# Attention with exact maxima: value products of two key tiles together, three score and three maximum banks, keys and values fetched in paced pieces

## The chip, the cores and the metric

One core of one Trainium2 chip runs the kernel. The metric is the time of one execution in microseconds (us). The kernel is the whole of a conditioned transformer block; the change is inside its attention stage.

## What is computed

Two sequences of 2048 rows of 512 channels pass through RMS norm with a conditioned shift and scale, 16-head attention (32 channels a head, rotary positions, no mask), and a gated feed-forward part, all float32:

```
qkv = h @ w_qkv + b_qkv
q, k = _rope(q), _rope(k)                  # heads of 32
attn = softmax(q k^T / sqrt(32)); out = attn @ v
x = x + out @ w_ao + b_ao
```

## The kernel before

Stage A writes rotated queries and keys (as a high and a low part that add up) and values to DRAM. Stage B, `stage_b` (line 472), is the attention; C and D are the output projection and the feed-forward part. B works in 32 **units** (`UNITS`): a unit is one group of four heads (`GH`, eight groups) and one block of 512 queries, four units to a group. A unit has 16 key tiles (`kt`) of 128 keys, and a loop of four rounds holds eight units written out (`run`, line 535).

For each tile and head PE makes a **score** matmul (`scores`, line 792: 128 keys by 512 queries into a bank of `ps_s`), ScalarE takes its exponential into the ring `pt` (line 656, eight tiles, `RING`), and four matmuls of 32 columns side by side, one per head, make the **value products** (PV, line 844) into `ps_o`. Softmax's maxima are made one unit ahead: a **maximum** matmul (line 767) gives 128 queries by 512 keys into a bank of `ps_m`, and VectorE reduces it (line 717). So a unit has 64 scores and 64 maxima, in the order `ORDER` = "smsmmsms" per key tile (s a score, m a maximum), and PV behind each such eight. There are `LEAD` = 2 score banks and `EARLY` = 4 maximum banks, one bank for `ps_o` and one for `ps_d`. A score waits until the exponential two before it is done (`p_ready`), a maximum until the reduction four before it is done (`max_done`).

The denominators are sums over all keys. POOL adds the ring's tiles into `acc` in pairs: `first_pair` (line 681) adds tiles 0 and 1; for the other seven pairs (`PAIRS`) `fold_pair` issues a DMA that adds the even tile onto the odd one inside the ring (line 688, 1 MB), when PV of the odd tile is done, and `add_pair` adds that into `acc` when the DMA has landed (line 695). POOL's order in a unit is: first pair, last add of the unit before, fold 0, fold 1, add 0, fold 2, add 1, and so on to fold 6, add 5. ScalarE may write tile kt into the ring only when `slot_free` says so: the add of the pair that lay there is done (`pool_added`). PE turns `acc` into denominators behind PV of tile 7 of the next unit (line 776, `D_AT`); at tile 10 (`TURN`) it transposes the finished maxima (line 786), which go through DRAM into the queries' last rows for the next unit.

SP's queue issues in each unit (`body`): queries of the unit after next (three transfers, 0.75 MB), then in the first unit of a group two of the next group's three key transfers (1 MB each), in the second the third, in the third the values (1 MB); then the output, the denominators, the maxima and the reciprocals.

## Time and profile before

| | us |
|---|---|
| median of three runs | 3688.61 (3687.13 to 3688.67) |
| the profiled execution | 3684.44 |
| its span, first to last instruction | 3682.6 |
| PE busy | 3247.0 (88%) |
| VectorE, POOL, ScalarE busy | 2028.4, 1660.1, 1573.8 |
| mean granted TensorE clock | 0.933 |

PE is TensorE's matmuls, PEld its weight loads, DVE VectorE, ACT ScalarE. b_ names are stage B's: b_s and b_m are the score and maximum banks, b_o the value products, b_d the denominators, b_pt the ring, b_acc the sums. A bracket behind an instruction is the idle time of its engine before it and what ended it. A value product of one key tile is eight instructions, which the timeline shows as one row.

### The profile page before, as it was taken

What the parts mean: (1) busy time and instruction counts of PE and PEld (TensorE: products, weight loads), DVE (VectorE), ACT (ScalarE), POOL (GpSimd) and SP (SyncE); (2) the same over time, 40 slices, a digit from 0 to 9 for tenths busy, and PEclk for the clock granted to TensorE, in tenths of its full rate; (3) what the DMA queues carried; (4) which work ended last, traced back from release to release, by engine and by line L of the source; (5) the groups of instructions that cost most, each with busy time, mean ns of one, the idle gap of its engine ahead of it and who ended that gap; (6) DMA issues with size and microseconds to landing.
All of it is one profiled execution on the core that took longest, in us unless ns stands there. A gap on an engine that the chain in (4) does not pass through costs nothing. (4 is left out here: it accounts for less than half of the span.)

```text
span 3682.6 us, 53143 instructions
## 1 busy us (share of the span) xinstructions
PE 3247.0 (88%) x15180; PEld 2087.6 (57%) x15180; DVE 2028.4 (55%) x3254; ACT 1573.8 (43%) x2848; POOL 1660.1 (45%) x732
## 2 busy tenths in 40 slices
PE   5888699999998998989999997444799999799999
PEld 5666544444444444444444443333588888688887
DVE  2878587777777776768777765434321222321222
ACT  1343226666666666657666664233211111211111
POOL 0222228877777777778877777655100000100000
PEclk9999869999999999999999998767899999899999
DMA  4444548887887878878887876654421120421210
GB/s 163 143 142 143 141 102 180 168 177 164 182 178 163 178 167 174 178 168 183 170 169 170 183 169 138 187 183 160 160 92 46 55 81 12 149 92 46 84 53 23
DMA packets 177578, 507.93 MB, mean 138 GB/s; under 512 B 25338, under 2 KB 42858, under 8 KB 143086
## 3 DMA queue, kind: packets, MB, share of 16 engines
q0 software_dynamic: 36240, 248.53, 33.1%
q1 hardware_dynamic: 130580, 233.58, 21.6%
q10 hardware_dynamic: 10512, 22.81, 1.9%
q8 instruction: 121, 1.98, 0.2%
q14 instruction: 125, 1.02, 0.1%
HBM read 175.18 MB, written 93.62 MB: 73 GB/s over the span
## 5 line engine op out<-in xcount | busy, mean ns | idle before, releaser
L717 DVE TENSOR_REDUCE b_mpart<-b_m 128x1 f32<-128x512 f32 x2136 | 1328.5, 684 | 480.3 <-PE b_m L767 476.0
L656 ACT ACTIVATE b_pt<-b_s 128x512 f32<-128x512 f32 x2048 | 1116.5, 596 | 625.4 <-PE b_s L792 492.7
L695 POOL TENSOR_TENSOR b_acc<-b_acc,b_pt 128x2048 f32<-128x2048 f32 x225 | 1040.4, 4624 | 352.2 <-DMA b_pt<-b_pt 350.8
L792 PE MATMUL b_s<-b_qs,b_ks 98*128 98x512 f32 x2050 | 904.2, 441 | 91.5 <-ACT b_pt L656 80.4
L792 PEld LDWEIGHTS b_s<-b_qs,b_ks 98*128 98x128 f32 x2050 | 393.7, 192 | 752.1 <-ACT b_pt L656 669.5
L767 PE MATMUL b_m<-b_ks,b_qs 96*128 96x512 f32 x2136 | 794.9, 419 | 20.9 <-issue 20.6
L844 PE MATMUL b_o<-b_pt,b_vg 128*32 128x512 f32 x4096 | 557.5, 617 | 0.0
L767 PEld LDWEIGHTS b_m<-b_ks,b_qs 96*128 96x128 f32 x2136 | 424.2, 199 | 96.4 <-DVE b_mpart L717 26.3
L1229 DVE SCALAR_TENSOR_TENSOR d_uf<-d_a,keep_chan,d_sg 128x512 f32<-128x512 f32 x128 | 96.1, 751 | 578.2 <-PE d_a L1257 578.2
L1181 POOL DMA_DIRECT2D d_raw<-in_w_fc x32 | 24.0, 755 | 592.1 <-POOLq L1106 495.7
L1200 ACT ACTIVATE d_sg<-d_g,keep_chan 128x512 f32<-128x512 f32 x128 | 88.0, 688 | 420.0 <-PE d_g L1257 420.0
L1203 ACT ACTIVATE d_u_hi<-d_uf 128x512 fp32r<-128x512 f32 x128 | 80.9, 632 | 433.8 <-DVE d_uf L1229 433.8
L1257 PE MATMUL d_g<-d_h_hi,d_w_hi 128*128 128x512 f32 x512 | 201.1, 393 | 45.8 <-DVE d_w_lo L1218 45.8
L341 POOL TENSOR_TENSOR a_qc<-a_q,early_cos 128x512 f32<-128x512 f32 x64 | 92.4, 1444 | 328.2 <-ACT a_q L307 297.3
L688 POOL DMA_DIRECT2D b_pt<-b_pt x224 | 201.5, 919 | 44.0 <-PE b_o L844 40.4
L1257 PE MATMUL d_g<-d_h_lo,d_w_hi 128*128 128x512 f32 x512 | 200.8, 392 | 0.0
L1257 PE MATMUL d_g<-d_h_hi,d_w_lo 128*128 128x512 f32 x512 | 200.8, 392 | 0.0
L1257 PE MATMUL d_a<-d_h_hi,d_w_hi 128*128 128x512 f32 x512 | 199.2, 389 | 0.0
L1257 PE MATMUL d_a<-d_h_hi,d_w_lo 128*128 128x512 f32 x512 | 199.2, 389 | 0.0
L1270 PE MATMUL d_y<-d_w_hi,d_u_hi 128*128 128x512 f32 x512 | 199.2, 389 | 0.0
L1270 PE MATMUL d_y<-d_w_hi,d_u_lo 128*128 128x512 f32 x512 | 199.2, 389 | 0.0
L1270 PE MATMUL d_y<-d_w_lo,d_u_hi 128*128 128x512 f32 x512 | 199.2, 389 | 0.0
(130 smaller groups left out, 3606.3 us busy)
## 6 DMA issues: line engine op xcount, KB each, us to landing
b_pt<-b_pt POOLq DMA_DIRECT2D x225, 1024.0 KB, 8.0
b_ks<-scratch_qk_hi SPq DMA_DIRECT2D x18, 1024.0 KB, 13.8
b_qs<-scratch_qk_hi SPq DMA_DIRECT2D x68, 256.0 KB, 6.0
scratch_qk_hi<-a_q_hi SPq DMA_DIRECT2D x64, 256.0 KB, 2.4
scratch_qk_lo<-a_q_lo SPq DMA_DIRECT2D x64, 256.0 KB, 2.8
d_h_hi<-scratch_h_hi SPq DMA_DIRECT2D x16, 1024.0 KB, 7.4
d_h_lo<-scratch_h_lo SPq DMA_DIRECT2D x16, 1024.0 KB, 9.6
d_y<-scratch_y SPq DMA_DIRECT2D x16, 1024.0 KB, 7.9
```

Of the source, the lines that this page charges most:

```text
L341: pool.tensor_tensor(qc[:, t % 2, :], q[:, t % 2, :], cos[:, bass.ds(it * TB, TB)], ALU.mult).then_inc(qc_ready, 1)
L656: act.activation(pt[:, kt % RING, h, :], ps_s[:, i % LEAD, :], ACT.Exp, scale=SCALE).then_inc(p_ready, 1)
L688: pool.dma_start(pt[:, kt % RING, :, :], pt[:, (kt - 1) % RING, :, :], accum_op=ALU.add).then_inc(pair_in[(PAIRS * j + n) % 2], 16)
L695: pool.tensor_tensor(acc[slot][:], acc[slot][:], pt[:, (2 * n + 3) % RING, :, :], ALU.add).then_inc(pool_added, 1)
L717: dve.tensor_reduce(mpart[slot][:, i // 4, i % 4:i % 4 + 1], ps_m[:, i % EARLY, :], AX.X, ALU.max).then_inc(max_done, 1)
L767: pe.matmul(ps_m[:, i % EARLY, :], qs[qslot][0:KR, h, s * P:(s + 1) * P], ks[kslot][0:KR, h, k * TB:(k + 1) * TB], start=True, stop=True). ...
L792: pe.matmul(ps_s[:, i % LEAD, :], ks[kslot][0:QR, h, kt * P:(kt + 1) * P], qs[qslot][0:QR, h, :], start=True, stop=True).then_inc(st_done, 1)
L844: last = pe.matmul(ps_o[h * HD:(h + 1) * HD, 0, :], vg[kslot][:, kt, h * HD:(h + 1) * HD], pt[:, kt % RING, h, :], start=kt == 0, stop=kt ...
L1200: act.activation(sg[:, f % 2, :], ps_g[:, f % 2, :], ACT.Silu, bias=chan[:, t:t + 1]).then_inc(sg_ready, 1)
L1229: dve.scalar_tensor_tensor(uf[:, f % 2, :], ps_a[:, f % 2, :], chan[:, t:t + 1], sg[:, f % 2, :], ALU.add, ALU.mult).then_inc(uf_ready, 1)
L1257: last = pe.matmul(ps[:, f % 2, :], w[:, f, t, k, :], h[s][:, k, :], start=i == 0, stop=i == 3 * KT - 1)
L1270: last = pe.matmul(ps_y[:, i, :], u[:, f % 2, i * P:(i + 1) * P], w[:, f, :], start=f == 0 and n == 0, stop=f == NF - 1 and n == 2)
```

## The change

1. PV of an even tile is left for the odd one: PE runs through sixteen scores and maxima, then makes both tiles' value products.
2. `LEAD` 2 to 3, `EARLY` 4 to 3. `bank(i)` gives item i of a unit its bank (i mod 3, and bank 1 for item 63), `before(i)` the item that had the bank last.
3. POOL issues fold 0 of a unit ahead of the last add of the unit before.
4. `slot_free`: an even tile's slot is free when the fold that read it has landed (`pair_in`), without waiting for the add; in the first unit of eight, where the pair belongs to the unit before, it still waits for the add.
5. Keys and values come in pieces of half a megabyte (two heads' keys, or eight tiles' values): `load_piece` gives unit j pieces 3(j mod 4) to 3(j mod 4) + 2 of eight; the first goes out when PV of three tiles of the unit is done, the second at six, the third behind the maxima. The output's store moves ahead of them.

```diff
@@ -465,8 +465,18 @@
 PAIRS = NK // 2 - 1
 ADDS = PAIRS + 1
 RING = 8
-LEAD = 2
-EARLY = 4
+LEAD = 3
+EARLY = 3
+def bank(i):
+    return i if i < 0 else 1 if i % 64 == 63 else i % 64 % 3
+def before(i):
+    return {0: -4, 1: -1, 2: -2, 63: 61}.get(i, i - 3)
 def stage_b(nc, io, keep, scratch):
@@ -543,12 +553,22 @@
             sp.sem_inc(d_out, 16)
             sp.sem_inc(r_out, 16 * GH)
-            def load_keys(G, i, r):
+            def load_keys(G, i, r, half):
                 src = qk_hi if r != 1 else qk_lo
-                sp.dma_start(f32(ks[i][r * HD:(r + 1) * HD, :, :]), src[1, G]).then_inc(k_in[i], 16)
-
-            def load_values(G, i):
-                sp.dma_start(vg[i][:], scratch["v"][G]).then_inc(v_in[i], 16)
+                heads = slice(GH // 2 * half, GH // 2 * (half + 1))
+                sp.dma_start(f32(ks[i][r * HD:(r + 1) * HD, heads, :]), src[1, G][:, heads, :]).then_inc(k_in[i], 16)
+            def load_values(G, i, half):
+                part = slice(NK // 2 * half, NK // 2 * (half + 1))
+                sp.dma_start(vg[i][:, part, :], scratch["v"][G][:, part, :]).then_inc(v_in[i], 16)
+            def load_piece(j, G, i, step):
+                piece = 3 * (j % 4) + step
+                if piece < 6:
+                    load_keys(G, i, piece // 2, piece % 2)
+                elif piece < 8:
+                    load_values(G, i, piece % 2)
             def load_queries(G, c, i):
                 for r, src in enumerate((qk_hi, qk_hi, qk_lo)):
...
@@ -594,17 +616,15 @@
                 sp.wait_ge(st_done, STEPS * (u + 1))
                 load_queries((2 * pair + (j + 2) // 4) % NG, (j + 2) % 4, (j + 2) % 4)
                 nG, ni = (2 * pair + j // 4 + 1) % NG, (j // 4 + 1) % 2
-                if j % 4 == 0:
-                    load_keys(nG, ni, 0)
-                    load_keys(nG, ni, 1)
-                if j % 4 == 1:
-                    load_keys(nG, ni, 2)
-                if j % 4 == 2:
-                    load_values(nG, ni)
                 G, c = (2 * pair + (j + 7) // 4 + NG - 2) % NG, (j + 3) % 4
                 store_output(u, G, c)
+                sp.wait_ge(pv_done, NK * u + RING - 1 + 3)
+                load_piece(j, nG, ni, 0)
+                sp.wait_ge(pv_done, NK * u + RING - 1 + 6)
+                load_piece(j, nG, ni, 1)
                 spread_denominators(u)
                 load_maxima(u + 1, (j + 1) % 2, (j + 1) % 4)
+                load_piece(j, nG, ni, 2)
                 store_reciprocals(u, G, c)
             run(sp, body)
...
@@ -635,11 +655,17 @@
                 act.wait_ge(d_out, 16 * (u + 1))
                 act.activation(d_sb[:], ps_d[:, 0, :], ACT.Copy).then_inc(d_read, 1)
-            def slot_free(u, kt):
+            def slot_free(u, kt, pair, j):
                 act.wait_ge(pv_done, NK * u + kt + 1)
                 old = (kt - RING) % NK
-                if old >= 2:
+                if old >= 2 and old % 2 == 0:
+                    g = PAIRS * (j if kt >= RING else j - 1) + old // 2 - 1
+                    if g >= 0:
+                        act.wait_ge(pair_in[g % 2], 16 * (PAIRS * 4 * pair + g // 2 + 1 + g % 2))
+                    else:
+                        act.wait_ge(pool_added, added(u - 1, old // 2 - 1))
+                elif old >= 2:
                     act.wait_ge(pool_added, added(u if kt >= RING else u - 1, old // 2 - 1))
                 else:
                     act.wait_ge(pool_added, ADDS * u + ADDS + 1)
@@ -649,11 +675,11 @@
             def body(u, pair, j):
                 for kt in range(NK):
-                    slot_free(u, kt)
+                    slot_free(u, kt, pair, j)
                     for h in range(GH):
                         i = GH * kt + h
                         act.wait_ge(st_done, STEPS * (u + 1) + i + 1)
-                        act.activation(pt[:, kt % RING, h, :], ps_s[:, i % LEAD, :], ACT.Exp,
+                        act.activation(pt[:, kt % RING, h, :], ps_s[:, bank(i), :], ACT.Exp,
                                        scale=SCALE).then_inc(p_ready, 1)
                         if kt == 0 and h == LEAD - 1:
                             read_products(u)
@@ -696,8 +722,8 @@
             def body(u, pair, j):
                 first_pair(u, j % 2)
+                fold_pair(u, j, pair, 0)
                 add_pair(u - 1, j - 1, pair, PAIRS - 1, (j + 1) % 2)
-                fold_pair(u, j, pair, 0)
                 for n in range(1, PAIRS):
                     fold_pair(u, j, pair, n)
                     add_pair(u, j, pair, n - 1, j % 2)
@@ -714,7 +740,7 @@
             def maxima(n, slot, lo, hi):
                 for i in range(lo, hi):
                     dve.wait_ge(max_ps, ITEMS * n + i + 1)
-                    dve.tensor_reduce(mpart[slot][:, i // 4, i % 4:i % 4 + 1], ps_m[:, i % EARLY, :], AX.X, ALU.max).then_inc(max_done, 1)
+                    dve.tensor_reduce(mpart[slot][:, i // 4, i % 4:i % 4 + 1], ps_m[:, bank(i), :], AX.X, ALU.max).then_inc(max_done, 1)
             def finish_max(n, slot):
                 dve.wait_ge(max_done, ITEMS * (n + 2))
@@ -763,8 +789,8 @@
                 for i in range(lo, hi):
                     h, s, k = i // 16, i // 4 % 4, i % 4
-                    pe.wait_ge(max_done, ITEMS * (n + 1) + i + 1 - EARLY)
-                    pe.matmul(ps_m[:, i % EARLY, :], qs[qslot][0:KR, h, s * P:(s + 1) * P],
+                    pe.wait_ge(max_done, ITEMS * (n + 1) + before(i) + 1)
+                    pe.matmul(ps_m[:, bank(i), :], qs[qslot][0:KR, h, s * P:(s + 1) * P],
                               ks[kslot][0:KR, h, k * TB:(k + 1) * TB], start=True, stop=True).then_inc(max_ps, 1)
             def denominators(u, slot):
@@ -779,7 +805,7 @@
             def operands(j, pair):
                 pe.wait_ge(q_in[j % 4], 48 * (2 * pair + j // 4 + 1))
-                pe.wait_ge(k_in[j // 4 % 2], 48 * (pair + j // 8 + 1))
+                pe.wait_ge(k_in[j // 4 % 2], 96 * (pair + j // 8 + 1))
             def turn_max(n):
                 pe.wait_ge(mneg_ready, n + 1)
@@ -788,8 +814,8 @@
             def scores(n, kslot, qslot, i):
                 kt, h = i // GH, i % GH
-                pe.wait_ge(p_ready, STEPS * (n + 1) + i + 1 - LEAD)
-                pe.matmul(ps_s[:, i % LEAD, :], ks[kslot][0:QR, h, kt * P:(kt + 1) * P], qs[qslot][0:QR, h, :],
+                pe.wait_ge(p_ready, STEPS * (n + 1) + before(i) + 1)
+                pe.matmul(ps_s[:, bank(i), :], ks[kslot][0:QR, h, kt * P:(kt + 1) * P], qs[qslot][0:QR, h, :],
                           start=True, stop=True).then_inc(st_done, 1)
             for i in range(SUB):
@@ -835,15 +861,18 @@
                     if kt == TURN:
                         pe.wait_ge(d_read, u + 2)
                         turn_max(u + 1)
-                    if kt == 0:
+                    if kt % 2 == 0:
+                        continue
+                    if kt == 1:
                         pe.wait_ge(o_read, u + 1)
                         if j % 4 == 0:
-                            pe.wait_ge(v_in[kslot], 16 * (pair + 1))
-                    pe.wait_ge(p_ready, STEPS * (u + 1) + GH * (kt + 1))
-                    for h in range(GH):
-                        last = pe.matmul(ps_o[h * HD:(h + 1) * HD, 0, :], vg[kslot][:, kt, h * HD:(h + 1) * HD],
-                                         pt[:, kt % RING, h, :], start=kt == 0, stop=kt == NK - 1)
-                    last.then_inc(pv_done, 1)
+                            pe.wait_ge(v_in[kslot], 32 * (pair + 1))
+                    for n in (kt - 1, kt):
+                        pe.wait_ge(p_ready, STEPS * (u + 1) + GH * (n + 1))
+                        for h in range(GH):
+                            last = pe.matmul(ps_o[h * HD:(h + 1) * HD, 0, :], vg[kslot][:, n, h * HD:(h + 1) * HD],
+                                             pt[:, n % RING, h, :], start=n == 0, stop=n == NK - 1)
+                        last.then_inc(pv_done, 1)
                     if kt == D_AT:
                         denominators(u, (j + 1) % 2)
```

**Order of the instructions, PE, at an even tile's end** (L791/L792 and in the change L817/L818 are scores, L766/L767 and L792/L793 maxima, L844 and L873 value products; ISA rows set up a wait). Before:

```order
L767 MATMUL b_m<-b_ks,b_qs 128x512
L791 ISA
L792 MATMUL b_s<-b_qs,b_ks 128x512
L842 ISA
L844 MATMUL b_o<-b_pt,b_vg 32x512 x4
L791 ISA
L792 MATMUL b_s<-b_qs,b_ks 128x512
L766 ISA
L767 MATMUL b_m<-b_ks,b_qs 128x512
```

Of the change, from an even tile's last score to the next tile's first maximum:

```order
L793 MATMUL b_m<-b_ks,b_qs 128x512
L817 ISA
L818 MATMUL b_s<-b_qs,b_ks 128x512
L817 ISA
L818 MATMUL b_s<-b_qs,b_ks 128x512
L792 ISA
L793 MATMUL b_m<-b_ks,b_qs 128x512
```

and at the odd tile's end:

```order
L818 MATMUL b_s<-b_qs,b_ks 128x512
L871 ISA
L873 MATMUL b_o<-b_pt,b_vg 32x512 x4
L871 ISA
L873 MATMUL b_o<-b_pt,b_vg 32x512 x4
L817 ISA
L818 MATMUL b_s<-b_qs,b_ks 128x512
```

The value products between the two tiles have gone behind those of the odd tile; scores and maxima keep their order.

**POOL, at a unit's start** (L681/L707 the first pair, L688/L714 a fold, L695/L721 an add). Before:

```order
L681 TENSOR_TENSOR b_acc<-b_pt 128x2048
L693 ISA
L694 ISA
L695 TENSOR_TENSOR b_acc<-b_acc,b_pt 128x2048
L686 ISA
L688 DMA b_pt<-b_pt 128x2048
L686 ISA
L688 DMA b_pt<-b_pt 128x2048
```

Of the change:

```order
L707 TENSOR_TENSOR b_acc<-b_pt 128x2048
L712 ISA
L714 DMA b_pt<-b_pt 128x2048
L719 ISA
L720 ISA
L721 TENSOR_TENSOR b_acc<-b_acc,b_pt 128x2048
L712 ISA
L714 DMA b_pt<-b_pt 128x2048
```

The first fold now stands ahead of the add, the second behind it.

## Rows read from the trace of the kernel before

**Rows 1.** The page: busy time by engine (section 1).
```profile
PE 3247.0 (88%) x15180; PEld 2087.6 (57%) x15180; DVE 2028.4 (55%) x3254; ACT 1573.8 (43%) x2848; POOL 1660.1 (45%) x732
```

**Rows 2.** Stretches: length, busy PE, PEld, DVE, ACT, POOL, clock, DMA share, GB/s.
```profile
887.80:938.60 50.80, 50.80 (x268) 24.52 (x267) 40.63 (x69) 35.66 (x67) 40.85 (x15) 1.00 0.80 167
1150.20:1211.30 61.10, 51.04 (x249) 24.79 (x248) 38.12 (x64) 33.65 (x63) 43.39 (x16) 0.89 0.84 173
...
519.00:2274.00 1755.00, 1663.78 (x8475) 802.37 (x8473) 1300.54 (x2174) 1145.03 (x2110) 1347.95 (x478) 0.97 0.83 172
```

**Rows 3.** Timeline of PE: start, us, instruction; one key tile, then the denominators.
```profile
1002.02 0.50 PE L792 MATMUL b_s<-b_qs,b_ks 98*128 98x512 f32 x1
1002.36 0.39 PE L767 MATMUL b_m<-b_ks,b_qs 96*128 96x512 f32 x1
1002.60 0.39 PE L792 MATMUL b_s<-b_qs,b_ks 98*128 98x512 f32 x1
...
1003.78 0.42 PE L792 MATMUL b_s<-b_qs,b_ks 98*128 98x512 f32 x1
1004.13 1.06 PE L844 MATMUL b_o<-b_pt,b_vg 128*32 128x512 f32 x8
1005.13 0.50 PE L792 MATMUL b_s<-b_qs,b_ks 98*128 98x512 f32 x1
...
1032.23 1.06 PE L844 MATMUL b_o<-b_pt,b_vg 128*32 128x512 f32 x8
1033.11 1.04 PE L776 MATMUL b_d<-b_acc,keep_ones 128*32 128x512 f32 x8
```

**Rows 4.** Waits of the stage, 520 to 2274 us: total, times, longest.
```profile
POOL b_acc L695 <- DMA b_pt<-b_pt: 348.5, 159, 9.1
...
ACT b_pt L656 <- POOL b_acc L695: 85.0, 22, 10.4
```

**Rows 5.** Timeline of POOL: an undisturbed unit's seam, then a stall.
```profile
899.60 0.87 POOL L688 DMA_DIRECT2D b_pt<-b_pt  x1
...
910.31 4.59 POOL L695 TENSOR_TENSOR b_acc<-b_acc,b_pt 128x2048 f32<-128x2048 f32 x1 [0.18 <-DMA b_pt<-b_pt]
...
1171.45 0.86 POOL L688 DMA_DIRECT2D b_pt<-b_pt  x1
...
1190.60 4.49 POOL L695 TENSOR_TENSOR b_acc<-b_acc,b_pt 128x2048 f32<-128x2048 f32 x1 [9.14 <-DMA b_pt<-b_pt]
1195.04 1.75 POOL L688 DMA_DIRECT2D b_pt<-b_pt  x2
```

**Rows 6.** DMA of the stage: queue, packets, MB, share; issues, us to landing.
```profile
q0 software_dynamic: 32000, 233.06, 66.3%
q1 hardware_dynamic: 35430, 66.52, 15.7%
...
b_pt<-b_pt POOLq DMA_DIRECT2D x223, 1024.0 KB, 8.0
```

**Rows 7.** Timelines of DVE, ACT and PEld over the tile of rows 3.
```profile
1002.79 2.49 DVE L717 TENSOR_REDUCE b_mpart<-b_m 128x1 f32<-128x512 f32 x4 [0.62 <-PE b_m L767]
...
1002.56 2.27 ACT L656 ACTIVATE b_pt<-b_s 128x512 f32<-128x512 f32 x4 [0.83 <-PE b_s L792]
...
1003.21 0.19 PEld L792 LDWEIGHTS b_s<-b_qs,b_ks 98*128 98x128 f32 x1 [0.19 <-ACT b_pt L656]
```

**Rows 8.** Timelines of DVE and PEld in the first maxima.
```profile
501.61 2.47 DVE L717 TENSOR_REDUCE b_mpart<-b_m 128x1 f32<-128x512 f32 x4
...
502.94 0.28 PEld L767 LDWEIGHTS b_m<-b_ks,b_qs 96*128 96x128 f32 x1 [0.31 <-DVE b_mpart L717]
```

**Rows 9.** Stretch at a low clock, and PE's timeline there.
```profile
480.00:520.00 40.00, 39.44 (x73) 19.59 (x76) 38.94 (x67) 3.35 (x7) 0.00 (x0) 0.50 0.29 62
...
518.83 0.63 PE L767 MATMUL b_m<-b_ks,b_qs 96*128 96x512 f32 x1
519.26 0.63 PE L792 MATMUL b_s<-b_qs,b_ks 98*128 98x512 f32 x1
```

More of the change, by code:

```diff
@@ L583, in _ @@
             load_queries(0, 0, 0)
-            for r in range(3):
-                load_keys(0, 0, r)
-            load_values(0, 0)
+            for half in range(2):
+                for r in range(3):
+                    load_keys(0, 0, r, half)
+            for half in range(2):
+                load_values(0, 0, half)
             sp.wait_ge(ones_ready, 1)
@@ L618, in _ @@
                 sp.wait_ge(q_in[i], 48 * (UNITS // 4 + 1))
-            sp.wait_ge(k_in[0], 48 * (NG // 2 + 1))
-            sp.wait_ge(v_in[0], 16 * (NG // 2 + 1))
+            sp.wait_ge(k_in[0], 96 * (NG // 2 + 1))
+            sp.wait_ge(v_in[0], 32 * (NG // 2 + 1))
         @block.scalar
```

## The prediction

> **What bounds the kernel now.** I read the page first: TensorE is busy in 88% of the span, no other engine in over 55% [rows 1]. The change touches only the attention stage, so I then asked for that stage: from 519 to 2274 us it is 1755 us for 32 units, **54.8 us each**, with PE at 95% of it, VectorE 74%, ScalarE 65%, POOL 77%, the DMA engines at 83% [rows 2]. Two units side by side tell what the 54.8 is made of [rows 2]: from 887.8 to 938.6 there is one unit in 50.8 us and PE never stops; from 1150.2 to 1211.3 the same unit takes 61.1 us, with the granted clock at 0.89. So 32 x (54.8 - 50.8) = 128 us are stalls, the rest is PE's own beat.
>
> The beat, in order of time [rows 3]: a score or maximum matmul every 0.23 us, 0.35 from the last score to the value products (PV), 1.00 from PV to the next score, and 0.34 instead of 0.23 to the matmul behind that. One key tile takes 1005.13 - 1002.02 = 3.11 us. Sixteen of them are 49.8; the denominators add 0.88 (1033.11 - 1032.23 [rows 3]) and the maximum's transpose 0.2: 50.8, as the undisturbed unit shows.
>
> The stalls: the waits of the stage put 85.0 us on ScalarE waiting for POOL's adds, 22 times, up to 10.4 us, and 348.5 us on POOL waiting for the folding DMA [rows 4]. The timeline of one shows why [rows 5]. The last fold of a unit is issued at 1171.45, its add starts at 1190.60: 19.2 us to land, where the median is 8.0 [rows 6]. In that stretch the SP queue has put out 0.75 MB of queries and 2 MB of keys. In the undisturbed unit of rows 2, which begins with queries alone, it is 899.60 to 910.31, 10.7 us. POOL stands idle for 9.14 us with the next unit's fold 0, long ready, queued behind that add; then it issues two folds at once (1195.04) and waits again. ScalarE's slot for key tile 6 is freed by that add alone, which ends at 1190.60 + 4.49 = 1195.09; this is the wait of 10.4 us [rows 4]. PE follows.
>
> **The change, part by part.** (1) PV of two key tiles together. Per two key tiles one passage in and out of PV falls away. One PV with its passage is 0.35 + 1.00 + 0.34 = 1.69 us. In the place of the first of two, scores and maxima now run on (two steps of 0.23), and its product costs, behind or ahead of the other, what the denominators cost behind a PV, 0.88 to 0.91 (I take 0.91): 1.69 - 0.46 - 0.91 = 0.3 saved. Two tiles by PE alone: 6.22 - 0.3 = **5.9 us**. That is the gain if nobody makes PE wait, 8 x 0.3 = 2.5 us a unit.
>
> (2) The maximum banks go from four to three, while eight maxima now come in one burst without the rest that PV gave. This is what I think decides the time, and it follows from four distances: VectorE starts a reduction 0.43 us after its matmul (1002.36 to 1002.79), reductions follow at (2.48 - 0.68) / 3 = 0.60 us [rows 7], and a matmul that waits for a bank starts 0.74 us after the reduction that frees it started (in the first maxima, where PE runs behind VectorE: reductions start at 501.61 and 502.21, and the weights of a waiting maximum at 502.94, 0.73 to 0.74 behind the second [rows 8]). ScalarE's are 0.45, 0.50 and 0.65 (1002.56 to 1003.21) [rows 7]. Put down from the first score at 0, matmuls at the beat of rows 3: m0 0.34, m1 0.80, m2 1.04, m3 1.51, m4 2.21, m5 2.67, m6 2.91, m7 3.37, the next score at 5.9; scores at 0, 0.57, 1.27, 1.74, 1.97, 2.44, 3.14, 3.61. Reductions d0 to d7: 0.77, 1.37, 1.97, 2.57, 3.17, 3.77 and on. m5 needs d2 + 0.74 = 2.71 (hardly late), m6 needs d3 + 0.74 = 3.31 instead of 2.91, m7 needs d4 + 0.74 = 3.91 instead of 3.77. So the last score stands at 4.14, PV at 4.49, 4.49 + 0.91 + 1.00 = 6.40; each late maximum also loads its weights uncovered, as the matmul behind PV does, 0.1 more (0.34 against 0.23). Between **6.38 and 6.50 I take 6.45 us** for two tiles: slower than 6.22. During the double PV VectorE has finished d7 by about 5.0 and idles, so nothing is made up. With four banks all these waits would vanish (m6 would need d2 + 0.74 = 2.71).
>
> The same walk for the three score banks: exps at 0.54, 1.04, 1.73, 2.22, 2.72; the latest demand is score 7, at 2.72 + 0.65 = 3.37, before its place at 4.14. So the third score bank costs nothing and covers PV (three exps are 1.8 us against 1.9 of PV). Banks are numbered so that items 63 and 1 have two banks instead of three: for the maxima m7 of tiles 8 and 9 then needs d5, 0.6 us later, once a unit. The transpose in the middle of a pair is hidden by the wait of m6.
>
> Unit without stalls: 8 x 6.45 + 0.9 + 0.6 = **53.1 us against 50.8: +2.3**.
>
> (3) Fold 0 goes ahead of the last add of the unit before, and even slots are freed when the fold that read them has landed rather than after the add. Fold 0 can be issued when PV of tile 3 is done, 2 x 6.45 = 12.9 us into the unit, and takes 0.9; the last fold goes out when PV of tile 15 is done, at about the unit's start, and beside queries alone lands 10.7 us later, so it is no longer the last to be waited for. The add ends at 12.9 + 0.9 + 4.6 = 18.4 us (4.6: rows 5). ScalarE needs it for tile 7, whose first score (28) is the second one behind three double tiles: 3 x 6.45 + 0.57 + 0.45 = 20.4 us, 2.0 us to spare. Tile 6 (score 24, at 12.9 + 2.44 + 0.45 = 15.8 us) now needs only the landing. Each us of landing past about 15.8 shows on PE.
>
> (4) Keys and values in eight half-megabyte pieces a group instead of four transfers, the first two of a unit behind PV of tiles 3 and 6, the third behind the maxima. The bytes stay. Nothing on SP is waited for before tile 10: its denominators come at tile 8, its maxima at 11, so the two new waits (tiles 3 and 6) hold up nothing behind them. Half pieces could cost more engine time: the SP queue takes 15.7% of 1755 us for 66.5 MB, 4.1 us per MB [rows 6]. The 1 MB of a unit could cost between nothing more and the same 4.1 us again (a half as dear as a whole), nearer to nothing, since half of that queue's bytes come in 256 KB transfers already (1 of 2 MB a unit). Two queues' 45 us plus 4.1 are 92% of a unit, so either is hidden. The Trainium skill (DMA: Bandwidth & Descriptors, Rules for kernel authors) wants at least 1 MiB in a DMA for full rate and so speaks against the halves; by it the pieces would load the queue more, and in the sum nothing would change unless the folds land later.
>
> Stalls that stay: in the first of eight units the even slots still wait for the add (tile 6 at 15.8 us, add done at 18.4: 2.6 / 8 = 0.3 us a unit). Between 0 and the 4.0 of now I take this 0.3, since the three causes seen in [rows 5] (a 2 MB burst, fold 0 queued behind, the add as the release) are each taken away.
>
> **Sum.** 32 x (53.1 + 0.3 - 54.8) = -45 us. The profiled execution took 3684.4; the median of the runs is 3688.6, 4.2 more. 3688.6 - 45 = **3644 us**. The first maxima run on VectorE's 0.60 with three banks as with four ((0.74 + 0.43) / 3 = 0.39 us, and 0.53 with the 0.43 doubled for a halved clock, both under 0.60), and all other stages are as before.
>
> **Rivals.**
> - *Reductions keep up* and the pair takes 5.9: 8 x 5.9 + 0.9 + 0.2 = 48.3. The two DMA queues take (66.3 + 15.7)% of 54.8 = 45.0 us a unit [rows 6], 93% of that, so folds land later and some waits stay: 49.5, 32 x 5.3 = 170, 3519 us. Against it: it needs reductions at under 0.47 us, they come at 0.60. Chance 0.08.
> - *The stalls stay* (slower). If the last fold, now in the queue with fold 0, lands as late as before, ScalarE waits at tile 7 instead of 6. Then the longer beat is all there is: 32 x 2.3 = +74, 3762 us. It decides from 2.3 - 4.0, i.e. once more than 1.7 us of stalls a unit are left. For it: beside queries alone the last fold already takes 10.7 us, 2.7 above the median, and now a half megabyte of the unit before may still be in front of them. Against: the undisturbed unit of rows 2 began with queries too. Chance 0.11.
> - *The clock falls* (slower). From 480 to 520 us the weight loads of the maxima stood idle 0.31 of each 0.60 us for a reduction, and the granted clock was 0.50, the 1.2 GHz level [rows 8, 9]; a score then took its place every 0.43 us instead of 0.23 [rows 9]. A pair at that level costs 16 x 0.2 + 2 x 0.9 less the waits that it covers, about 4.4 us more. One pair in eight: 32 x 4.4 = 141 more, 3785 us; one in 25 eats the gain. Against: PE still works 5.9 of 6.45 us. The Trainium skill (TensorE: Matmul & The Clock Gate, A second HAM failure mode) tells of a kernel whose short waits on PSUM banks made the clock swing between its levels, which is this case's shape; here it is at 0.50 in the first maxima and part of the time in the stalled unit (0.89), while the undisturbed unit keeps 1.00 [rows 2]. Chance 0.04.
> - *It doesn't do what it says*, e.g. the pacing waits are already met (the count starts at 7): the wait asks 7 + 3, so they hold. Even then the keys only come as now. No chance of its own.
>
> **How the numbers follow.** The forecast has 0.77. Its own range: 6.38 to 6.50 a pair is -18 to +13 us, stalls of 0 to 1 us a unit -10 to +22: 3616 to 3679. For 8 in 10 I reach some way to both sides: **3590 to 3695**, which leaves out most of the two slow rivals and the fast one. Under 0.2%, 7 us, a change can't be told from none here. Faster: 0.77 + 0.08 less a tail of 0.04, **0.81**; same **0.04**; slower **0.15**.
>
> **What would show it.** Right: maxima's weight loads idle before two or three matmuls of eight, put down to VectorE; two tiles in 6.4 to 6.5 us; gaps of 5 to 10 us on PE behind ScalarE gone; fold landings under 14 us; DMA share about 85%. Wrong: pairs of 5.9 (my bank walk fails), ScalarE still waiting for POOL for 50 us or more (the reordering fails), or a granted clock under 0.95 in the stage.

## The result, and the profile after

| | before | changed |
|---|---|---|
| median of four runs, us | 3688.6 (3687.1 to 3689.7) | 3644.4 (3642.6 to 3647.2) |
| the profiled execution | 3684.4 | 3647.2 |
| its span | 3682.6 | 3645.4 |
| mean granted TensorE clock | 0.933 | 0.946 |

The ratio is 0.9901, with a 95% interval of 0.9878 to 0.9924: 44 us faster, against a forecast of 45.

The page of the changed kernel, busy time by engine, beside [rows 1]:

```profile
PE 3249.6 (89%) x15181; PEld 2092.3 (57%) x15181; DVE 2003.0 (55%) x3254; ACT 1590.4 (44%) x2848; POOL 1670.0 (46%) x732
```

There is nothing to see there: every engine does what it did. Stretches of the stage, with the columns of [rows 2], tell more; the first is the stage, the second one unit:

```profile
540.00:2240.00 1700.00, 1646.60 (x8378) 796.90 (x8376) 1261.19 (x2151) 1147.53 (x2086) 1350.68 (x474) 0.99 0.84 178
1000.00:1053.00 53.00, 51.91 (x267) 25.25 (x267) 39.86 (x69) 36.33 (x67) 42.71 (x15) 1.00 0.90 192
```

PE is busy in 97% of the stage, but an undisturbed unit now has PE idle for 1.1 of its 53.0 us, where before it had none in 50.8 [rows 2]. The timeline of PE, one pair of key tiles, against [rows 3] (start, us, instruction; L818 scores, L793 maxima, L873 value products, L802 denominators):

```profile
1001.70 1.92 PE L873 MATMUL b_o<-b_pt,b_vg 128*32 128x512 f32 x16
1003.55 0.50 PE L818 MATMUL b_s<-b_qs,b_ks 98*128 98x512 f32 x1
...
1006.34 1.01 PE L793 MATMUL b_m<-b_ks,b_qs 96*128 96x512 f32 x2
...
1007.45 0.50 PE L793 MATMUL b_m<-b_ks,b_qs 96*128 96x512 f32 x1
...
1008.12 1.92 PE L873 MATMUL b_o<-b_pt,b_vg 128*32 128x512 f32 x16
...
756.39 1.04 PE L802 MATMUL b_d<-b_acc,keep_ones 128*32 128x512 f32 x8
809.40 1.04 PE L802 MATMUL b_d<-b_acc,keep_ones 128*32 128x512 f32 x8
```

Two tiles take 1008.12 - 1001.70 = 6.42 us. The last two rows are one unit apart, 53.0 us, and the units between the loop's ends are all 53.0. Weight loads in the same pair:

```profile
1005.06 0.19 PEld L793 LDWEIGHTS b_m<-b_ks,b_qs 96*128 96x128 f32 x1 [0.29 <-DVE b_mpart L743]
...
1006.25 0.19 PEld L793 LDWEIGHTS b_m<-b_ks,b_qs 96*128 96x128 f32 x1 [0.17 <-DVE b_mpart L743]
1006.85 0.19 PEld L793 LDWEIGHTS b_m<-b_ks,b_qs 96*128 96x128 f32 x1 [0.41 <-DVE b_mpart L743]
...
1007.45 0.19 PEld L793 LDWEIGHTS b_m<-b_ks,b_qs 96*128 96x128 f32 x1 [0.30 <-DVE b_mpart L743]
```

These are maxima m3, m5, m6 and m7 of the eight; each waits for VectorE. m7 starts 1007.45 - 1003.55 = 3.90 us behind the first score. The waits of the stage (total, times, longest), beside [rows 4]:

```profile
PEld b_m L793 <- DVE b_mpart L743: 282.9, 903, 0.9
...
POOL b_acc L721 <- DMA b_pt<-b_pt: 140.9, 122, 3.3
...
ACT L682 <- issue: 20.0, 3, 7.2
...
ACT b_pt L682 <- POOL b_acc L721: 13.0, 4, 4.2
```

ScalarE's waits for POOL have gone from 85.0 us to 13.0, POOL's for its folds from 348.5 to 140.9, and waits of PE's weight loads for VectorE have come in. The seam between two units on POOL, against [rows 5]:

```profile
1059.30 0.86 POOL L714 DMA_DIRECT2D b_pt<-b_pt  x1
...
1064.44 4.86 POOL L707 TENSOR_TENSOR b_acc<-b_pt 128x2048 f32<-128x2048 f32 x1
1070.09 0.87 POOL L714 DMA_DIRECT2D b_pt<-b_pt  x1 [0.78 <-PE b_o L873]
1070.70 4.87 POOL L721 TENSOR_TENSOR b_acc<-b_acc,b_pt 128x2048 f32<-128x2048 f32 x1
```

The last fold goes out at 1059.30, fold 0 at 1070.09 with only PE's value products to wait for, and the last add follows without a wait. The queues' shares, against [rows 6]:

```profile
q0 software_dynamic: 32096, 233.85, 67.8%
q1 hardware_dynamic: 37046, 67.99, 15.4%
...
b_pt<-b_pt POOLq DMA_DIRECT2D x223, 1024.0 KB, 8.0
b_ks<-scratch_qk_hi SPq DMA_DIRECT2D x32, 512.0 KB, 5.1
```

A fold's median stays at 8.0 us. The SP queue took 15.4% of 1720 us for 68.0 MB, 3.9 us per MB where it was 4.1, so no cost of the halves is to be seen. The Trainium skill (DMA: Bandwidth & Descriptors, Rules for kernel authors) wants 1 MiB and more in a DMA for the most bandwidth. No run here measures a DMA's rate by itself, but the queue's engine time per MB did not rise.

### The profile page after: what moved, and what is told of

Its sections match the earlier page's. It is cut to its first block and busy times, and to the rows that moved or that the text cites. A ratio compares the mean times of both kernels' runs of the same rounds, so it can differ in the third digit from the quotient of the medians.

```text
span 3645.4 us, 53309 instructions
## 1 busy us (share of the span) xinstructions
PE 3249.6 (89%) x15181; PEld 2092.3 (57%) x15181; DVE 2003.0 (55%) x3254; ACT 1590.4 (44%) x2848; POOL 1670.0 (46%) x732
## 5 line engine op out<-in xcount | busy, mean ns | idle before, releaser
L743 DVE TENSOR_REDUCE b_mpart<-b_m 128x1 f32<-128x512 f32 x2136 | 1306.2, 683 | 469.7 <-PE b_m L793 469.6
L682 ACT ACTIVATE b_pt<-b_s 128x512 f32<-128x512 f32 x2048 | 1132.5, 601 | 540.2 <-PE b_s L818 504.0
L721 POOL TENSOR_TENSOR b_acc<-b_acc,b_pt 128x2048 f32<-128x2048 f32 x225 | 1054.7, 4687 | 143.5 <-DMA b_pt<-b_pt 143.3
L793 PE MATMUL b_m<-b_ks,b_qs 96*128 96x512 f32 x2136 | 899.5, 452 | 51.7 <-issue 20.1
L818 PE MATMUL b_s<-b_qs,b_ks 98*128 98x512 f32 x2051 | 821.9, 417 | 23.3 <-ACT b_pt L682 19.6
L793 PEld LDWEIGHTS b_m<-b_ks,b_qs 96*128 96x128 f32 x2136 | 413.4, 194 | 371.6 <-DVE b_mpart L743 312.4
L818 PEld LDWEIGHTS b_s<-b_qs,b_ks 98*128 98x128 f32 x2051 | 391.1, 191 | 322.4 <-issue 208.1
L873 PE MATMUL b_o<-b_pt,b_vg 128*32 128x512 f32 x4096 | 492.5, 598 | 0.0
L714 POOL DMA_DIRECT2D b_pt<-b_pt x224 | 195.3, 872 | 205.7 <-PE b_o L873 188.4
L873 PEld LDWEIGHTS b_o<-b_pt,b_vg 128*32 128x32 f32 x4096 | 106.8, 109 | 247.7 <-issue 184.2
L1286 PE MATMUL d_a<-d_h_lo,d_w_hi 128*128 128x512 f32 x512 | 199.2, 389 | 0.0
```

Source lines behind the costliest of these rows:

```text
L682: act.activation(pt[:, kt % RING, h, :], ps_s[:, bank(i), :], ACT.Exp, scale=SCALE).then_inc(p_ready, 1)
L714: pool.dma_start(pt[:, kt % RING, :, :], pt[:, (kt - 1) % RING, :, :], accum_op=ALU.add).then_inc(pair_in[(PAIRS * j + n) % 2], 16)
L721: pool.tensor_tensor(acc[slot][:], acc[slot][:], pt[:, (2 * n + 3) % RING, :, :], ALU.add).then_inc(pool_added, 1)
L743: dve.tensor_reduce(mpart[slot][:, i // 4, i % 4:i % 4 + 1], ps_m[:, bank(i), :], AX.X, ALU.max).then_inc(max_done, 1)
L793: pe.matmul(ps_m[:, bank(i), :], qs[qslot][0:KR, h, s * P:(s + 1) * P], ks[kslot][0:KR, h, k * TB:(k + 1) * TB], start=True, stop=True).th ...
L818: pe.matmul(ps_s[:, bank(i), :], ks[kslot][0:QR, h, kt * P:(kt + 1) * P], qs[qslot][0:QR, h, :], start=True, stop=True).then_inc(st_done, 1)
```

## The experiments

The changed kernel agrees with the forecast in its beat, but a sum can come out right by two errors. So the parts were run apart, and then what was left. Ratios are to the kernel before on the same chip, with 95% intervals; a unit's length is the time from one unit's denominators to the next one's. The kernel before took 3685.4 (beside e1 to e4), 3684.0 (e5 to e8) and 3688.7 us (e9 to e12 and the changed kernel's own runs 3688.6), so differences of medians across these are good to some 4 us. e1's maxima leave out half of the keys, so its output is another one; only its time is of use. All others compute the whole block.

| kernel | us | ratio |
|---|---|---|
| e5 pieces alone | 3691.2 | 1.0016 [1.0000, 1.0032] |
| e12 slots alone | 3728.1 | 1.0107 [1.0071, 1.0144] |
| e2 fold 0 first alone | 3649.9 | 0.9903 [0.9881, 0.9924] |
| e9 fold 0 first, slots | 3612.4 | 0.9796 [0.9762, 0.9830] |
| e6 fold 0 first, pieces | 3611.3 | 0.9795 [0.9756, 0.9833] |
| e3 fold 0 first, slots, pieces | 3579.9 | 0.9716 [0.9700, 0.9732] |
| e4 merging and banks alone | 3693.6 | 1.0019 [1.0002, 1.0036] |
| the whole change | 3644.4 | 0.9901 [0.9878, 0.9924] |
| e10 whole change, banks 2 and 4 | 3622.2 | 0.9827 [0.9793, 0.9861] |
| e7 whole change, other order | 3579.9 | 0.9721 [0.9686, 0.9756] |
| e1 whole change, half reductions | 3582.7 | 0.9720 [0.9701, 0.9740] |
| e8 as e3, no loop | 3550.5 | 0.9636 [0.9602, 0.9670] |
| e11 as e7, no loop | 3548.8 | 0.9625 [0.9592, 0.9659] |

### Which resource sets the pair of tiles: e1, e10, e7

e1 shortens the reductions:

```diff
-                                       scale=SCALE).then_inc(p_ready, 1)
+                                       scale=SCALE / 64).then_inc(p_ready, 1)
...
-                    dve.tensor_reduce(mpart[slot][:, i // 4, i % 4:i % 4 + 1], ps_m[:, bank(i), :], AX.X, ALU.max).then_inc(max_done, 1)
+                    dve.tensor_reduce(mpart[slot][:, i // 4, i % 4:i % 4 + 1], ps_m[:, bank(i), 0:TB // 2], AX.X, ALU.max).then_inc(max_done, 1)
```

> The changed kernel, but VectorE reduces only 256 of the 512 columns of each maximum matmul (so the maxima are those of half the keys, and the exponent is scaled by 1/64 to stay finite): the same instructions, shorter reductions. Theory (three banks and a reduction every 0.60 us hold PE up at the sixth to eighth maximum of a pair): the reductions then follow at about 0.34 us, no maximum waits, two key tiles fall from the 6.42 us measured after the change to 5.9, and a unit from 53.0 to 48.5 to 50.6, where folds start to hold it: 3500 to 3575 us. Rival (the second pair of value products or the three score banks set the 6.42): two tiles stay at 6.3 to 6.4 us, 3630 to 3645 us.

Measured: 3582.7 us, 8 above the theory's range. PE's timeline, three value products behind one another:

```profile
1005.25 1.92 PE L873 MATMUL b_o<-b_pt,b_vg 128*32 128x512 f32 x16
...
1011.17 1.93 PE L873 MATMUL b_o<-b_pt,b_vg 128*32 128x512 f32 x16
...
1017.00 1.92 PE L873 MATMUL b_o<-b_pt,b_vg 128*32 128x512 f32 x16
```

and from the waits of its stage:

```profile
PE b_s L818 <- DMA b_qs<-scratch_m: 30.0, 19, 2.3
...
PEld b_m L793 <- DVE b_mpart L743: 15.1, 31, 0.5
```

The first pair, 5.92 us, has the maxima's transpose in it; the second, without it, takes 5.83. In the changed kernel both kinds take 6.42. Nothing is altered in time but the reductions' length, and the weight loads' waits for VectorE fell from 282.9 to 15.1 us. So VectorE behind three banks sets the 6.42. The fastest units are 48.6 us, but most are 50 to 54: with the shorter beat the maxima's way through DRAM and the folds come late.

e10 puts two score and four maximum banks back, in a kernel that still merges:

```diff
-LEAD = 3
-EARLY = 3
...
+LEAD = 2
+EARLY = 4
...
-                    pe.wait_ge(max_done, ITEMS * (n + 1) + before(i) + 1)
...
+                    pe.wait_ge(max_done, ITEMS * (n + 1) + i + 1 - EARLY)
...
-                pe.wait_ge(p_ready, STEPS * (n + 1) + before(i) + 1)
...
+                pe.wait_ge(p_ready, STEPS * (n + 1) + i + 1 - LEAD)
```

> The changed kernel with the banks put back: two for scores, four for maxima, value products still two tiles together. Theory by the same walk: no maximum waits any more, but a score now waits for the exponential two before it; score 4 starts at 1.73 + 0.65 = 2.37 instead of 1.97 and everything behind it moves, 6.3 to 6.4 us for two tiles instead of 6.42; the extra 0.6 us of the bank numbering goes: 52.0 to 52.5 a unit, 3610 to 3635 us. Weight loads of scores wait for ScalarE, those of maxima for nobody. Rival (the four maximum banks are all that counts): 5.9 for two tiles, 3590 us or less.

Measured: 3622.2 us, units of 52.0. Its PE timeline:

```profile
999.68 1.92 PE L863 MATMUL b_o<-b_pt,b_vg 128*32 128x512 f32 x16
...
1003.29 0.42 PE L808 MATMUL b_s<-b_qs,b_ks 98*128 98x512 f32 x1
1003.91 0.50 PE L808 MATMUL b_s<-b_qs,b_ks 98*128 98x512 f32 x1 [0.20 <-ACT b_pt L672]
...
1006.02 1.92 PE L863 MATMUL b_o<-b_pt,b_vg 128*32 128x512 f32 x16
```

The pair is 6.34 us, and score 4 starts 0.62 us after score 3 instead of 0.23, released by ScalarE: the other side binds, where the walk put it. Two tiles with separate value products take 2 x 3.11 = 6.22 us [rows 3], and merged ones 5.83 when nobody waits (e1). So either split of six banks costs more than merging brings; 3 and 3 takes 22 us more than 2 and 4.

e7 keeps 3 and 3 and changes one string:

```diff
-        ORDER, TURN = "smsmmsms", 10
+        ORDER, TURN = "msmssmsm", 10
```

> The changed kernel with one string altered: the order of scores and maxima in a tile is msmssmsm instead of smsmmsms. The first maximum then starts at 0 behind the value products instead of 0.34, two maxima never stand side by side within a tile, and the last one of a pair is the last matmul before the value products, so that it may start at 0.54 + 4 x 0.60 + 0.74 = 3.68 us, its natural place. Theory: two tiles 5.9 to 6.1 us instead of 6.42, units of 49 to 50.5 with some waits for folds, 3560 to 3595 us. Rival (the three banks bind whatever the order): 6.3 or more for two tiles, 3625 us or above.

Measured: 3579.9 us, 64.5 less than the changed kernel. Its PE timeline:

```profile
1003.47 1.92 PE L873 MATMUL b_o<-b_pt,b_vg 128*32 128x512 f32 x16
1005.33 0.50 PE L793 MATMUL b_m<-b_ks,b_qs 96*128 96x512 f32 x1
...
1009.43 1.92 PE L873 MATMUL b_o<-b_pt,b_vg 128*32 128x512 f32 x16
```

The pair is 5.96 us. Three banks nearly suffice if the maxima are spread over the pair and VectorE is started at once behind the value products. The maxima's weight loads still wait 217.9 us in the stage for VectorE, against 282.9, but the pair is only 0.13 us longer than e1's.

### What took the stalls: e2, e5, e12, e6, e9, e3

e2 is one swap in POOL's order:

```diff
-                add_pair(u - 1, j - 1, pair, PAIRS - 1, (j + 1) % 2)
                 fold_pair(u, j, pair, 0)
+                add_pair(u - 1, j - 1, pair, PAIRS - 1, (j + 1) % 2)
```

> The kernel before with one part of the change alone: fold 0 issued ahead of the last add of the unit before. Theory (the stalls came from fold 0 being queued behind an add that waits for the landing of the last fold): most of the 4.0 us of stalls a unit go, PE keeps its own beat of 50.8: 50.8 to 51.5 a unit, 3565 to 3590 us, faster than the whole change. Rival (the 2 MB burst of keys delays the landings, and the order only moves the wait): units that begin with keys still stall by 8 us or more, 3650 us or above.

Measured: 3649.9 us, 60 above the theory's range and at the rival's bound: the swap alone is a third of what it brings with its two companions (e3 below). ScalarE's timeline tells the two reasons:

```profile
589.29 3.47 ACT L656 ACTIVATE b_pt<-b_s 128x512 f32<-128x512 f32 x6 [1.54 <-POOL b_acc L695]
...
803.19 1.09 ACT L656 ACTIVATE b_pt<-b_s 128x512 f32<-128x512 f32 x2 [7.86 <-POOL b_acc L695]
```

The first row comes back in nearly every unit, since the last add now stands behind fold 0 and ends just after ScalarE wants tile 6 (584.27 + 4.88 = 589.15); units are 51.5 us instead of 50.8. That is what freeing the slot at landing is good for. The second row is a fold that still lands late. It lies in unit 5 (counted from 0), which begins with 1 MB of keys, and not in unit 4, where the 2 MB go out; e9 shows why.

e5 is the pieces alone (`load_keys`, `load_values`, `load_piece`, the two waits on `pv_done` and the counts of the waits on keys and values, as in the change):

> The kernel before with the paced half-megabyte pieces alone. Theory (every unit that stalls has the last fold landing late and fold 0 queued behind it; the burst is only one of the causes): the long stalls of units that begin with 2 MB of keys shrink, those of the others stay or grow a little, as every unit but the fourth now has pieces: 53.5 to 55.5 us a unit, 3640 to 3700 us. Rival (the burst alone makes the stalls): 51.5 a unit or less, 3590 us or less.

Measured: 3691.2 us, within the theory's range, no gain. The waits of its stage, against [rows 4]:

```profile
POOL b_acc L705 <- DMA b_pt<-b_pt: 375.4, 167, 8.1
ACT b_pt L666 <- POOL b_acc L705: 87.7, 50, 4.6
```

As much waiting as before (87.7 against 85.0 us), in 50 waits instead of 22, none over 4.6. Pacing by itself spreads the stalls over the units.

e12 is `slot_free` alone:

```diff
...
-                if old >= 2:
+                if old >= 2 and old % 2 == 0:
+                    g = PAIRS * (j if kt >= RING else j - 1) + old // 2 - 1
+                    if g >= 0:
+                        act.wait_ge(pair_in[g % 2], 16 * (PAIRS * 4 * pair + g // 2 + 1 + g % 2))
+                    else:
+                        act.wait_ge(pool_added, added(u - 1, old // 2 - 1))
+                elif old >= 2:
...
```

> The kernel before with the slots freed at landing alone. Theory (the landing of the last fold and the fold 0 queued behind it are what is late; ScalarE's slots only tell when it shows): the stalls move by a tile, not away: 53.5 to 55.5 a unit, 3645 to 3700 us. Rival (the slots' rule is the main part of the gain): 3620 us or less.

Measured: 3728.1 us, slower than theory and rival had it. ScalarE's timeline at the start of unit 4, where 2 MB of keys go out:

```profile
752.18 1.08 ACT L662 ACTIVATE b_pt<-b_s 128x512 f32<-128x512 f32 x2 [7.74 <-DMA b_pt<-b_pt]
...
756.90 1.09 ACT L662 ACTIVATE b_pt<-b_s 128x512 f32<-128x512 f32 x2 [1.79 <-POOL b_acc L701]
```

Tile 6 starts at the landing, and one tile later ScalarE stops again for the add. Over the stage it waits 65.0 us for the folds' DMA and 61.5 for POOL, 126.5 together against 85.0. Before, a long unit is followed by an undisturbed one (62.5, 50.8, 58.9, 50.8 us for the fourth to seventh, counted between denominators); here the same four are all disturbed (60.5, 55.6, 57.3, 53.9). It looks as if the long stop used to let POOL catch up for the next unit; that is argued, no run isolates it.

e6 and e9 add one each of the two to the swap.

> Fold 0 first and paced pieces, without freeing the slots at landing; separate value products, two and four banks. It tells what the slots' rule adds to the version with all three (3580 us, 50.8 us a unit beside three back edges of 10 us). Theory (fold 0 alone left stalls of 8 to 10 us in the units with 2 MB or 1 MB of keys, which the pieces break up): 51.5 a unit as with fold 0 alone, no stall between the back edges, 3595 to 3615 us. Rival (the slots' rule does it, pieces nothing): units with stalls of 4 us and more, 3630 us or above.

> Fold 0 first and slots freed at landing, but keys and values in bursts of 2, 1 and 1 MB as before; separate value products, two and four banks. Against 3580 us with the pieces too. Theory (a landing later than about 15.8 us into the unit shows on PE, and beside 2 MB of keys the last fold takes up to 19): the units that begin with 2 MB of keys stall by 3 to 6 us, all others take 50.8: 3595 to 3625 us. Rival (with fold 0 first and free slots the burst is hidden): 3575 to 3585 us, the pieces buy nothing.

Measured: 3611.3 and 3612.4 us. e6 has units of 51.4 to 54.0 between the loop's ends, and no stop of PE there over 2 us. e9 has 50.7 to 51.6, and four of 56.0 to 59.5, each with one stop of PE of 3.6 to 5.5 us. The size is as expected (3 to 6), the place is not: the stops lie in units 5, 13, 21 and 29, which begin with 1 MB of keys, one unit behind those that begin with 2 MB. The one in unit 5:

```profile
797.02 1.08 ACT L662 ACTIVATE b_pt<-b_s 128x512 f32<-128x512 f32 x2 [6.39 <-DMA b_pt<-b_pt]
```

POOL in units 4 and 5:

```profile
751.12 4.57 POOL L701 TENSOR_TENSOR b_acc<-b_acc,b_pt 128x2048 f32<-128x2048 f32 x1 [8.26 <-DMA b_pt<-b_pt]
...
779.89 0.85 POOL L694 DMA_DIRECT2D b_pt<-b_pt  x1
...
797.09 4.55 POOL L701 TENSOR_TENSOR b_acc<-b_acc,b_pt 128x2048 f32<-128x2048 f32 x1 [4.85 <-DMA b_pt<-b_pt]
```

and SP's queue at the start of unit 5:

```profile
778.38 1.18 SPq L548 DMA_DIRECT2D b_ks<-scratch_qk_hi  x1
```

In unit 4 the last fold went out at 723.21, ahead of the queries and the 2 MB of keys (723.77 to 728.6), and nothing stopped. It was unit 4's own fold 0 (735.79) that took 15.3 us beside the burst, and POOL was late for the rest of the unit. So the last fold went out at 779.89, behind the queries and the 1 MB of keys of unit 5, and POOL took it up 17.2 us later. The times are the trace's; that the lateness is handed on in this way is our reading of them, and e6, where the pieces take the bursts away, agrees with it.

e3 has all three, and the value products, banks and beat of before:

> The kernel before with fold 0 first, the slots freed at landing and the paced pieces, but value products of each tile by themselves and two score and four maximum banks as before. Theory: only the loop's three back edges (6 to 7 us each) are left of the stalls: 50.8 to 51.2 a unit, 3560 to 3580 us, 65 to 85 us faster than the changed kernel, because merging with three banks costs 2.2 us a unit. Rival (merging pays, and the whole change needs its parts together): 3645 us or more.

Measured: 3579.9 us, as the theory has it. All units are 50.7 to 51.6 but those at the loop's ends. Its stage:

```profile
540.00:2180.00 1640.00, 1611.46 (x8378) 777.39 (x8377) 1283.77 (x2151) 1129.08 (x2087) 1349.26 (x476) 0.99 0.88 185
```

Against the kernel before on its own chip the swap takes 35 us off (e2), swap and pieces 73 (e6), swap and slots 76 (e9), all three 105 (e3). Without the swap the pieces add 7 us (e5) and the slots 39 (e12).

### Merging on its own: e4

This is the kernel before with the banks and the merged value products of the change, nothing else.

> The kernel before with the other half of the change: value products of two tiles together and three and three banks, nothing else. Theory: two tiles take 6.4 us, a unit without stalls 53.0; the slower PE gives POOL 2.2 us more a unit, so part of the old stalls vanish by themselves: 53.3 to 54.8 a unit, 3640 to 3690 us. Rival (stalls add to the longer beat as they stood): 57 us a unit, 3755 us.

Measured: 3693.6 us, 4 above the theory's range and far from the rival's. Its waits:

```profile
POOL b_acc L705 <- DMA b_pt<-b_pt: 257.4, 151, 8.9
...
ACT b_pt L666 <- POOL b_acc L705: 89.2, 27, 11.0
```

Undisturbed units are 53.0 here too, and more of them are undisturbed, as the slower beat gives POOL time; the long stalls stay, now mostly one unit behind the 2 MB of keys (9.9 us in units 5 and 21, 11.0 in unit 13). Added to e3 the same edit costs 3644.4 - 3579.9 = 64.5 us, 2.0 a unit.

### What was left: e8, e11

In the changed kernel the 32 units are 53.0 us but for three of 60.8 to 62.0, those over the loop's back edge, where every engine branches back to start the next round. ScalarE's timeline there:

```profile
945.65 1.28 ACT L682 ACT_TABLE_LOAD   x1 [5.89 <-issue]
```

It stands 5.89 us without a semaphore to wait for, and then loads its table again. The waits of the stage before [rows 4] had such a row too:

```profile
ACT L656 <- issue: 8.7, 2, 5.8
```

e8 is e3 with the loop of rounds written out, e11 is e7 with the same:

```diff
-            with eng.Fori(0, UNITS // 8) as pair:
+            for pair in range(UNITS // 8):
```

> The version without merging (3580 us) with the loop of four rounds written out, so that no engine branches back. Theory (ScalarE stands for 6 to 7 us at each back edge with no semaphore to wait for, and its table is loaded anew for 1.3 us, which with the low clock behind it costs 10 us a round): the three edges go, 3545 to 3560 us. Rival (fetching new instructions costs as much as branching back): 3575 to 3585 us, or slower if the straight code has to be fetched all the time.

> The changed kernel with the order msmssmsm and the loop written out. Theory: the 10 us a round that the back edges cost go, as in the version without merging (3580 to 3550 us): 3545 to 3555 us; the shorter beat of PE (49.7 us in its best units) is eaten by waits for the maxima's way through DRAM, which at 88% DMA share comes up to 2 us late. Rival (without the edges the merged version's shorter beat shows): 3535 us or less.

Measured: 3550.5 and 3548.8 us, 29.4 and 31.1 less than with the loop. e8's denominators at the place of the first edge, then e3's:

```profile
900.94 1.04 PE L792 MATMUL b_d<-b_acc,keep_ones 128*32 128x512 f32 x8
...
952.34 1.04 PE L792 MATMUL b_d<-b_acc,keep_ones 128*32 128x512 f32 x8
```

```profile
899.58 1.04 PE L792 MATMUL b_d<-b_acc,keep_ones 128*32 128x512 f32 x8
...
959.89 0.61 PE L792 MATMUL b_d<-b_acc,keep_ones 128*32 128x512 f32 x4
```

51.4 against 60.3 us. The branch and the reloading of the table go together in both, so how much of the cost is either's is not shown. These two are the fastest kernels of the study, 134 and 140 us below the kernel before on their own chips; they can't be told from each other. e11's best units are 49.8 us, but others take up to 53.1, with PE waiting up to 1.8 us for the maxima from DRAM, as the theory had it; e8's are 50.7 nearly throughout.

## Why the prediction was right

- **PE's beat and the stalls.** 54.8 us a unit were read as 50.8 of beat and 4.0 of stalls. e8 shows the beat bare: 50.7. Of the 128 us of stalls, though, the three back edges were a part that the prediction took for POOL's: e8 prices them at 29 us, and the trace before had them too, as waits on "issue" of ScalarE. The waits were read by their totals by releaser, and these were among the small ones.
- **The walk over the banks.** Forecast m7 at 3.91, pair 6.38 to 6.50, taken as 6.45, unit 53.1. Measured 3.90, 6.42, 53.0. The two late maxima named were late; m3 and m5 wait too, at little cost. Merged products by PE alone take 5.83 (e1), a little less than the 5.9 of the prediction. The cause is shown from three sides (e1 5.83, e7 5.96, e10 6.34 with the wait on ScalarE's side). "With four banks all these waits would vanish" holds for the maxima, but needed the clause that two score banks then bind.
- **The double lead of items 63 and 1** was put at 0.6 us a unit. It was not run by itself, but the timeline of the changed kernel shows it, behind the denominators of 756.39:

```profile
761.88 0.50 PE L793 MATMUL b_m<-b_ks,b_qs 96*128 96x512 f32 x1 [0.47 <-DVE b_mpart L743]
```

  This is m7 of tiles 8 and 9, 4.51 us behind the pair's first score (757.37) instead of 3.90: 0.6 us, in every unit. The unit's sum (8 x 6.42 + 0.9 = 52.3, 53.0 measured) leaves 0.7.
- **The stalls go.** The three causes were named and said to be taken away one each. That holds for the whole (ScalarE's waits for POOL 85.0 to 13.0 us), and e2, e5 and e12 show more than was said: none of the three does it alone, one is harmful alone. The picture of [rows 5], in which the unit with the 2 MB stalls longest, holds for the kernel before; in e2, e4 and e9 the longest stalls lie in the unit behind it.
- **Stalls that stay**, 0.3 us a unit from the slots' old rule once in eight units: mis-sized. ScalarE shows that wait (13.0 us in 4 waits), but of it only 0.4 to 1.8 us once in eight units reach PE, 0.1 a unit. The three units over a back edge, though, are 24.8 us longer than 53.0 together, some 22 of it the edge: 0.7 a unit that was not in the sum.
- **The sum.** -45 us forecast, -44 measured by the medians, -37 between the two profiled executions. In the profiles, from the first denominators on, 31 units went from 55.0 to 53.8 us each, 38 us. The sum took a residue of 0.3 where 0.8 a unit is to be seen, so the agreement of the medians to 1 us is partly luck; the profile's own -37 is the fairer test, 8 us off.
- **Rivals.** The low clock did not come: granted 0.99 in the stage, 1.00 in an undisturbed unit, with PE idle for 1.1 of 53 us in short waits. By the Trainium skill's account (TensorE: Matmul & The Clock Gate, A second HAM failure mode) a kernel that cycles through PSUM banks made the clock swing by such short waits; in this kernel's undisturbed units they did not. The stalls did not stay, and reductions did not keep up.
- **DMA share** was forecast at about 85%: 0.84. Fold landings under 14 us: of the folds that POOL had to wait for, the slowest was taken up 10.6 us behind its issue, where it was 19.2 in [rows 5].

## What to carry to other kernels

Merging two short phases to save their passages takes away the rest that the consumer between them used: walk the banks through the merged stretch with three distances from the trace (producer to consumer, consumer to consumer, consumer to freed bank) before believing the saving, and then try the order within the stretch, which here was worth all that the merge had lost (64.5 us), and no more: merged and separate products end at the same time, with the loop (3579.9 both) and without it. An in-order queue that waits for a late transfer should have all ready work ahead of that wait; letting downstream engines go on earlier without this here only moved the stop and made it worse (e12). And test a bundle of edits part by part: here one half was worth 105 us and the other cost 65.

## What the runs showed of the hardware that was not expected

- A loop's back edge made the unit over it 8 to 11 us longer (60.8 to 62.0 against 53.0 in the changed kernel, 60.0 to 61.4 against 50.8 in e3). In the changed kernel ScalarE stands 5.9 to 7.2 us there and its table load takes 1.28 us more; PE stands 4.7 us and then works at the 1.2 GHz level for a while (0.83 granted on average from 940 to 960 us). Straight code of four times the length had no such stops and took 29 to 31 us less over three edges.
- Half-megabyte transfers were no dearer than whole ones on the SP queue (3.9 against 4.1 us per MB), and landed in 5.1 us at the median where 1 MB took 14.2 beside the same folds. The halves were paced and the whole ones came in bursts, so the landing times are not those of size alone.
